# x's diagonals written by DMA, x's sums in h's rest banks, sums chained into h's rows, and four recurrence steps per turn of VectorE's loop

## The reference

```python
# 1. a recurrence over 128 time steps, batch 8, width 128, from h0 = cond_1024
xw = einsum('ntd,dh->nth', x, Wx) + b
h  = tanh(xw_t + h @ Wh)              # step by step
# 2. latent attention, 16 heads, causal, on h, added to x
# 3. a gated scan over time (adaptive layer) with softplus and tanh gates
# 4. six layers of local attention (16 heads of 64, window 32) and a gated feed-forward net
```

## Time and profile before

| | us |
|---|---|
| median of 3 runs | 3380.21 (3375.91 to 3382.81) |
| the profiled execution's own time | 3381.28 |
| its span | 3379.5 |
| PE busy | 2812.6 (83%) |
| VectorE busy | 2809.4 (83%) |
| ACT busy | 2171.9 (64%) |
| POOL busy | 2593.7 (77%) |

### The profile page before, as it was taken

One profiled execution on the slowest core, in us unless ns is written; L12 is line 12 of the kernel. 1 busy time (PEld: TensorE's weight loads), 2 busy tenths in 40 slices (PEclk: granted clock), 3 DMA queues, 4 the chain that ended last, 5 costly groups with the idle time before them and its releaser, 6 DMA issues.

```text
span 3379.5 us, 54177 instructions
## 1 busy us (share of the span) xinstructions
PE 2812.6 (83%) x12991; PEld 1717.5 (51%) x13101; DVE 2809.4 (83%) x8061; ACT 2171.9 (64%) x4492; POOL 2593.7 (77%) x2804
## 2 busy tenths in 40 slices
PE   5777778777787877878777788969999999999997
PEld 2333333333333333333333336746767777777676
DVE  5999999999999999999999994337777777777875
ACT  4666666666666666666666663336666666666665
POOL 8888888888888888888888881038778778778773
PEclk9999999999999999999999998879999999999999
DMA  1000000000000000000000002000010101000000
GB/s 33 0 0 0 0 0 0 0 0 0 0 0 0 0 0 0 0 0 0 0 0 0 0 0 73 1 1 1 0 36 0 36 0 36 0 32 4 0 0 7
DMA packets 21860, 21.97 MB, mean 7 GB/s; under 512 B 6334, under 2 KB 19396, under 8 KB 21060
## 3 DMA queue, kind: packets, MB, share of 16 engines
q1 hardware_dynamic: 21828, 21.55, 2.0%
HBM read 21.02 MB, written 0.52 MB: 6 GB/s over the span
## 4 chain that ended last, share of the span: by engine, by line
DVE 54%; PE 21%; issue 15%; ACT 4%; POOL 3%; DVEq 2%; SPq 0%; DMA 0%; POOLq 0%; ACTq 0%
DVE bank L1017 13%; PE bank L1322 5%; DVE bank L1012 3%; DVE bank L989 3%; DVE rot_s L1235 3%; DVE sq L989 3%; DVE rot_c L1235 3%; DVE ss L1238 3%; PE bank L1564 2%; DVE qT L998 2%; PE bank L1642 2%; DVE fix_trace L1083 2%; PE bank L1426 2%; PE bank L1616 2%; DVE sq L1075 2%
## 5 line engine op out<-in xcount | busy, mean ns | idle before, releaser
L1017 DVE TENSOR_REDUCE bank<-qkv_w 128x2 f32<-128x766 f32 (+1 forms) x768 | 912.7, 1219 | 120.6 <-issue 64.9
L739 ACT COPY qkv_w<-bank 128x512 f32<-128x512 f32 x258 | 218.2, 846 | 356.9 <-PE bank L1322 356.9
L667 POOL TENSOR_TENSOR qk<-rot_c,rot_s 128x512 f32<-128x512 f32 x192 | 256.8, 1337 | 207.8 <-DVE rot_s L1235 207.8
L1322 PE MATMUL bank<-diag_h,w_part 128*128 128x512 f32 x1024 | 307.2, 421 | 118.2 <-DVE bank L1012 106.9
L585 POOL TENSOR_TENSOR diag_h<-eye,part 128x512 fp32r<-128x512 f32 x384 | 393.9, 1040 | 0.0
L578 POOL TENSOR_TENSOR qkv_w<-b,offset 128x512 f32<-128x512 f32 x258 | 269.1, 1043 | 160.4 <-ACT b L721 150.0
L1327 PE MATMUL bank<-kT,wx 128*128 128x512 f32 x516 | 277.0, 618 | 136.3 <-ACT b L721 136.3
L1322 PE MATMUL bank<-diag_x,w_part 128*128 128x512 f32 x1032 | 385.6, 495 | 0.0
L1337 PE MATMUL bank<-qT,wh 128*128 128x256 f32 (+1 forms) x768 | 254.6, 467 | 95.6 <-DVE qT L998 95.6
L674 POOL TENSOR_TENSOR rs<-rs,halfs 128x8 f32<-128x8 f32 x192 | 320.1, 1667 | 16.0
L716 ACT ACTIVATE diag_x<-eye,X 128x128 fp32r<-128x128 f32 x1036 | 327.7, 389 | 1.4 <-DVE X L1110 1.4
(11 more groups left out here) (237 smaller groups left out, 6697.5 us busy)
## 6 DMA issues: line engine op xcount, KB each, us to landing
qkv_w<-in_L_ffn_Wqkv SPq DMA_DIRECT2D x6, 1536.0 KB
o_w<-in_L_ffn_Wo SPq DMA_DIRECT2D x6, 512.0 KB
w<-in_L_ffn_W SPq DMA_DIRECT2D x6, 341.0 KB
b<-in_L_ffn_b SPq DMA_DIRECT2D x6, 341.0 KB
w<-in_L_ffn_W SPq DMA_DIRECT2D x6, 128.0 KB
x_tok<-in_x SPq DMA_DIRECT2D x1, 512.0 KB
masks<-in_masks SPq DMA_DIRECT2D x1, 512.0 KB, 3.8
out<-o_fin SPq DMA_DIRECT2D x1, 512.0 KB, 3.2
```

The lines of the kernel that those rows point to most:

```text
L667: pool.tensor_tensor(o, c_, s_[:, :, ::-1, :], ALU.add).then_inc(rot_sum, 1)
L1017: return dve.tensor_reduce((sum_h, sum_x)[n][:, a:b], chain[n][:, a:b, 0:LINKS], AX_X, ALU.add)
L1322: return pe.matmul(dst, w_part[:, n, w], diag[n][:, d, a:b, :].rearrange("p n k -> p (n k)"), start=start, stop=stop or n == 0, skip_group ...
```

## The change

**x's diagonals by DMA.** ACT and POOL no longer make them. A ring of four slots in device memory holds, per slot, both parts' diagonal matrices for eight batch rows, 1 MB, cleared once with zeros from `o_fin`. In each step SyncE stores the 2 x 1024 elements of one later step of x onto the diagonals of a slot (a DMA with single elements of 4 bytes) and loads a half (512 KB, in 256 pieces of 2 KB) twice, each into its place in `diag_x` as soon as PE has done with it.

**Banks.** x's sums are made in banks 2 and 3, h's rest banks, when h's rests have been copied out of them. x's rests get a bank per half, 4 and 6. ACT reads a sum once into `guess_x` and once more, negated, into the rest bank, which takes the place of the product with `minus_eye`.

**Chained sums.** The bias is written once as the last link of x's rows; the result of x's fold is written as the last link of h's rows; folds read 384 in place of 383 links, and h's fold writes `pre` itself. The adds `xw` and `pre` go.

**Order and shares.** The triangle of h's batch rows 2, 3 moves from VectorE to ACT (`triangle_mid`). The lower diagonal of half 0 moves from ACT to POOL, that of half 1 from POOL to ACT. Both negated guesses of h are now POOL's (`minus_h`). PE makes all four products of half 0 before those of half 1.

**Loop.** VectorE's loop runs over 32 turns with four steps written out in each; the semaphore `rnn_op` is cleared once a turn.

```diff
+            def send_diagonals_x(step, slot):
+                for d in range(2):
+                    src = x_part[d][:, step, :] if isinstance(step, int) else x_part[d][:, bass.ds(step, 1), :].rearrange(
+                        "p a n -> p (a n)")
+                    dst = bass.AP(ring.tensor, (slot * P * 2 + d) * NB * D, [[2 * NB * D + 1, P], [D, NB], [1, 1]])
+                    sp.dma_start(dst, src.unsqueeze(2), allow_slow_non_contiguous=True).then_inc(diag_x_sent, 16)
+            def bring_diagonals_x(slot, half):
+                rows = slice(4 * half, 4 * half + 4)
+                sp.dma_start(diag[1][:, :, rows, :].bitcast(F32), ring[slot][:, :, rows, :]).then_inc(diag_x_ready[half], 16)
...
+            with sp.Fori(0, T // RING) as turn:
+                for u in range(RING):
+                    t = RING * turn + u
+                    sp.wait_ge(rest_ready[1], value(sp, 2 * t + 2))
+                    bring_diagonals_x((u + 1) % RING, 1)
+                    sp.wait_ge(rest_ready[1], value(sp, 2 * t + 3))
+                    bring_diagonals_x((u + 2) % RING, 0)
+                    sp.wait_ge(diag_x_sent, value(sp, 32 * t + 32 * RING))
+                    send_diagonals_x(value(sp, (t + RING) % T), u)
@@ POOL's loop @@
                 triangle(0, h_now[:], 1, tri_h_second)
                 pool.wait_ge(split_h, this)
-                for half in range(2):
-                    diagonal(0, 0, half, part[:, 0, 4 * half:4 * half + 4], diag_upper_h)
+                diagonal(0, 0, 0, part[:, 0, 0:4], diag_upper_h)
+                diagonal(0, 1, 0, part[:, 1, 0:4], diag_lower_h[0])
+                minus_h(0, counts[0])
+                diagonal(0, 0, 1, part[:, 0, 4:8], diag_upper_h)
                 pool.tensor_copy(hT[:, bass.ds(t, 1), :].rearrange("p a n -> p (a n)"), h_now[:]).then_inc(h_ready, 1)
-                diagonal(0, 1, 1, part[:, 1, 4:8], diag_lower_h[1])
-                pool.wait_ge(guess_placed, counts[1])
-                pool.tensor_tensor(adds[0][:, 4:8, :, 2], adds[0][:, 4:8, :, 1],
-                                   signs[:, 1:2].unsqueeze(2).to_broadcast([P, 4, D]), ALU.mult).then_inc(minus_placed[1], 1)
-                pool.wait_ge(rest_ready[1], counts[1])
-                diagonal(1, 1, 1, lower_x(around, 1), diag_x_ready[1])
+                minus_h(1, counts[1])
                 pool.wait_ge(x_scanned, this)
                 place_sums_x(0, counts[2])
                 place_sums_x(1, counts[3])
-                diagonal(1, 1, 0, lower_x(beyond, 0), diag_x_ready[1])
@@ ACT's loop @@
+            def triangle_mid():
+                for n in (2, 3):
+                    ins = act.activation(tri[0][:, n, :], upto[:], ACT.Copy, scale=h_now[:, n:n + 1])
+                ins.then_inc(tri_h_mid, 1)
             def take_sums_x(half, count):
+                act.activation(bank[:, REST_BANKS_X[half], :], sums_, ACT.Identity, bias=offset[:, 0:1],
+                               scale=-1.0).then_inc(less_guess, 1)
...
+                act.wait_ge(h_static, this)
+                triangle_mid()
                 place_guess_h(0, counts[0])
                 place_guess_h(1, counts[1])
                 act.wait_ge(split_h, this)
                 lower_h()
-                place_minus_h(counts[0])
                 place_rests_h(0, counts[0])
+                place_rests_h(1, counts[1])
                 act.wait_ge(sum_placed[1], counts[1])
+                act.wait_ge(rest_placed[1], counts[1])
                 take_sums_x(0, counts[2])
-                place_rests_h(1, counts[1])
                 take_sums_x(1, counts[3])
-                diagonals_x(around, 1)
                 act.wait_ge(x_scanned, this)
                 place_rests_x(0, counts[2])
-                diagonals_x(beyond, 0)
                 place_rests_x(1, counts[3])
@@ VectorE @@
-                return dve.tensor_reduce((sum_h, sum_x)[n][:, a:b], chain[n][:, a:b, 0:LINKS], AX_X, ALU.add)
+                return dve.tensor_reduce((pre, bias_at[0])[n][:, a:b], chain[n][:, a:b, :], AX_X, ALU.add)
...
-            with dve.Fori(0, T) as t:
+            with dve.Fori(0, T // UNROLL) as turn:
                 count[0] = 0
                 dve.sem_clear(rnn_op)
+                for u in range(UNROLL):
+                    t = UNROLL * turn + u
...
-                step(dve.tensor_scalar(xw[:], sum_x, rnn_b[:], None, ALU.add))
...
-                after(step(fold(0, 6, 8)))
-                after(tt(pre, xw[:], sum_h, ALU.add))
+                    after(n_h)
@@ PE's loop @@
-                sums_x(0, counts[2])
                 for half in range(2):
                     pe.wait_ge(diff_ready, counts[half])
+                    for d, made, count in ((0, diag_upper_h, counts[half]), (1, diag_lower_h[half], this)):
+                        pe.wait_ge(made, count)
+                        for w in range(2):
+                            ins = times(bank[:, REST_BANKS_H[half], :], 0, w, d, 4 * half, 4 * half + 4)
+                    ins.then_inc(rest_ready[0], 1)
+                for half in range(2):
+                    pe.wait_ge(rest_placed[0], quarters[half])
+                    sums_x(half, counts[2 + half])
                 offset_h()
+                for half in range(2):
+                    rests_x(half, counts[2 + half], landed)
```

More of the change, by code:

```diff
@@ L68 @@
 OFFSET = 12.0
-LINKS = 3 * D - 1
+UNROLL = 4
+RING = 4
 def constants():
@@ L237, in own @@
                                   **dict(zip(names[1:], shape[1:])))
-        sum_h, sum_x, pre = own(0, NB), own(0, NB), own(0, NB)
+        pre = own(0, NB)
         offset = sb("offset", [P, 2])
@@ L278, in program @@
         adds = [qkv_w[:, n, :].rearrange("p (n i c) -> p n i c", n=NB, c=3) for n in range(2)]
+        bias_at = [tile[:, :, D - 1, 2] for tile in adds]
         chain = [qkv_w[:, n, :].rearrange("p (n i) -> p n i", n=NB) for n in range(2)]
+        ring = nc.dram_tensor('diag_ring', (RING, P, 2, NB, D), F32, kind='Internal').ap()
         in_x = sem("in_x")
@@ L304, in program @@
         guess_placed = sem("guess_placed_h")
-        minus_placed = [sem("minus_placed_h%d" % half) for half in range(2)]
+        minus_placed = sem("minus_placed_h")
         diag_upper_h = sem("diag_upper_h")
         diag_lower_h = [sem("diag_lower_h%d" % half) for half in range(2)]
-        diag_x_ready = [sem("diag_upper_x"), sem("diag_lower_x")]
+        diag_x_ready = [sem("diag_x%d" % half) for half in range(2)]
+        zeros_ready = sem("zeros_ready")
+        diag_x_sent = sem("diag_x_sent")
+        ring_clear = sem("ring_clear")
         tri_h_first = sem("tri_h_first")
@@ new lines, in _, with placed_h @@
+                dve.sem_clear(rnn_op)
+                for u in range(UNROLL):
+                    t = UNROLL * turn + u
+                    this, two = value(dve, t + 1), value(dve, 2 * t)
+                    counts = [value(dve, two + n) for n in (1, 2, 3, 4)]
+                    quarters = [value(dve, 4 * t + n) for n in (1, 2, 3, 4)]
+                    def placed_h(m):
+                        dve.wait_ge(rest_placed[0], quarters[m])
+                        if m % 2 == 0:
+                            dve.wait_ge(minus_placed, counts[m // 2])
+                    placed_x(counts[0])
+                    n_x = step(fold(1, 0, 4))
+                    for half in range(2):
+                        difference_h(half, counts[half])
+                    placed_x(counts[1])
+                    fold(1, 4, 8).then_inc(x_scanned, 1)
+                    after(n_x)
+                    for m in range(4):
+                        placed_h(m)
+                        if m == 2:
+                            dve.wait_ge(x_scanned, this)
+                        n_h = step(fold(0, 2 * m, 2 * m + 2))
+                    after(n_h)
+                    tanh()
+                    open_step(value(dve, t + 2))
@@ L1339, in sums_h, with rests_x @@
                                  skip_group_check=True)
[L1341 removed]
+            def rests_x(half, count, landed):
                 a, b = 4 * half, 4 * half + 4
[L1343 removed]
+                at = bank[:, REST_BANKS_X[half], :]
                 rows = at.rearrange("p (n k) -> p n k", k=D)
                 pe.wait_ge(guessed, count)
[L1346 to L1347 removed]
+                pe.wait_ge(less_guess, count)
+                pe.matmul(rows, eye[:], guess_x[:, a:b, 0:D], start=False, stop=True, skip_group_check=True)
+                pe.wait_ge(diag_x_ready[half], landed)
                 for d in range(2):
[L1349 to L1351 removed]
+                    for w in range(2):
+                        ins = times(at, 1, w, d, a, b)
                 ins.then_inc(rest_ready[1], 1)
```

155 lines of the change are left out of this document (60 added, 95 removed).

## The result

The changed kernel takes **3302.0 us** (median of 4 runs, 3298.6 to 3307.7), beside 3381.5 for the kernel before on the same chip: ratio 0.976 [0.975, 0.978]. That is 79.5 us off, where 142 were forecast (143 less 1 for the start), and 2 us above the range. The sign was right; 62 us are missing.

The account below looks back on a forecast made before the run. VectorE, busy 94% of the loop, was taken to bound the kernel: 128 steps each 1.12 us shorter (143) off 3381.3, plus 1 for start and end, gave 3239, or 3238 us against the median; 8-in-10 range 3212 to 3300.

Parts of the forecast that it names:

- Off VectorE's path go the products by -eye: TensorE's products by -eye, 1.0 us a half, and diagonals leave other engines; worth nothing by itself, pays for x's longer line.
- x's side, 0.3 us to spare: x's longer line through ScalarE, GpSimd and TensorE: GpSimd's and ScalarE's work each ends 0.3 us before it is needed.
- The rival (3295): x's side or ScalarE takes over through negated copies and ten handovers 0.03 us worse: steps of 15.0, 3295 us; chance 0.20.
- VectorE's sum: VectorE's list in one step: adds, triangle, stall and turn save 1.33 us; 14.55 on average once its wait is counted.
- The wait for the guess: Before h's first difference, VectorE waits 0.26 us for ScalarE's guess in three steps of four.
- The turn: VectorE's loop turn comes once in four steps: gain 0.43 us in three of four, 0.32 on average.
- The negated copy: ScalarE's negated copy of x's guess, PSUM to PSUM: bounds 0.69 and 0.96 us, 0.69 taken.
- The DMA: Loads of 1 MB (3.1 us) and 2048 single-element stores (2) a step: 5 of 14.5 us, hidden, so 0.
- The start: Before the loop, clears and chained stores end near 45 us: 0 to 5 us once; +1 for start and end.
- The loop body: Rival: each of VectorE's 32 loop turns waits 0 to 2.3 us for an instruction block: 3275 us; chance 0.07.

Follow-up runs that it names:

- e1: The changed kernel with 4 matmuls added behind h's sums and 5 behind x's rests in each step: 3254.2 us, ratio 0.962.
- e11: The changed kernel with 2 matmuls added behind h's sums and 2 behind x's rests in each step: 3249.0 us, ratio 0.961.
- e8: The changed kernel with -guess again from TensorE's product with the negative identity, not from ScalarE's second copy: 3307.2 us, ratio 0.978.
- e9: e1 with the triangle of h's elements 2 and 3 back on VectorE: 3261.3 us, ratio 0.965.
- e7: e1 with one step in each turn of VectorE's loop instead of four: 3266.9 us, ratio 0.966.
- e3: The changed kernel without the loop's stores of 4-byte elements, fetches kept: 3303.4 us, ratio 0.977.
- e13: e6 without the loop's stores and fetches of x's diagonals, TensorE waiting for the first landing alone: 3232.9 us, ratio 0.956.
- e4: The changed kernel with the zeros of all four ring slots written before the loads of the attention's weights: 3294.9 us, ratio 0.975.
- e6: e1 and e4 together, against the changed kernel: 3241.8 us, ratio 0.959.

## Why the prediction was wrong, point by point

- **The clock: the step that failed.** Every duration in the sum was a row at full clock, and the earlier trace rows showed 1.00. The prediction wrote "Off VectorE's path go the products by -eye" and put the exchange at nothing. It was worth the clock: TensorE idled 32.0 us in the ten steps of the earlier trace rows, 3.2 of 15.67, in four pieces of at most 1.06; in the step shown above it is 1.72 + 1.13 + 0.72 = 3.6 of 14.53, although its last products ran at half rate. The price was 54 us, which e1 and e11 took back, and with the product back there was no stretch (e8). That matmuls with short idle times between groups can make the clock swing is in the Trainium skill ("TensorE: Matmul & The Clock Gate", A second HAM failure mode: psum-queue depth-cycling); the trace agrees, with idle times of 0.7 to 1.7 us between groups. It was the rule to weigh here, but it would not have settled the forecast: the kernel before idles between its groups too, 0.46 to 1.06, and its clock never fell in the loop.
- **x's side, 0.3 us to spare.** Right for neither engine: in a step of e1 ScalarE is done 0.55 us before it is wanted and GpSimd 0.1 (its triangles of x end at 1022.60, h's begins at 1022.70). That GpSimd has so little is the reason why the clock cost anything. The rival (3295) named the place that gave way, but held ten late handovers responsible. At full clock there were none (e1: VectorE's folds of x do not wait for ScalarE's copies); with the product back, its mechanism is real (e8, 14.93 beside its 15.0).
- **VectorE's sum.** Forecast 14.52 in three steps of four and 14.66 with the turn; e1 has 14.46 and 14.67, 14.516 on average against 14.55. The two adds and the stall ahead of h's folds are gone.
- **The wait for the guess.** 0.26 forecast. From x's fold to L1046 it is 1.93 us (1021.66 to 1023.59), against 1.67 for such a fold with nothing behind it: 0.26. e9 shows the other side: of the triangle's 0.33 this wait takes back all but 0.03 (0.07 by the prediction's terms), except in the turn's step.
- **The turn.** Gain 0.43 for VectorE alone, 0.14 of the step net of the wait; e7 measured 0.19.
- **The negated copy.** 0.69 taken, 0.65 measured, the value below both bounds.
- **The DMA.** 5 us of the queues' time a step forecast, 5.2 measured; hidden (e3, e13). The times to landing were too low: 6.1 us for a half and 5.4 for a store are the medians of the page after, where 3.8 and 3.3 were taken. The three of them in a row would be 17.6 us, over the 12 that were allowed; yet in the loop TensorE never waits for a fetch.
- **The start.** +1 us taken for start and end, 0 to 5 allowed, 8 measured. The mis-sized term is the end of the other slots' clears and chained stores: put near 45 us, the clears issued at 28.32 hold the stores until 42.22, these end at 51.9, and the fetch behind them is issued at 52.02. e4 took back 7, a part of it by the clock (see e6).
- **The loop body.** The count was right at four steps; its cost past the edge, bounded at 2.3 us a turn, is 3.9.

## What to carry to other kernels

Before work is taken off TensorE in a loop of short dependent steps, look at its idle times and at the granted clock: work that costs nothing on the path may be what keeps the clock up. A row at full clock is no promise for the kernel after the change. Where the clock falls for short stretches, look where in the step they begin and put a few cheap matmuls into every gap that precedes one; filling one gap of two gained 0 and 14 us here, filling both thinly gained 53. And unroll only as far as the loop body stays loaded: from four steps to eight the turn went from 0.2 us to 4.

## What the runs showed of the hardware that was not expected

- Stretches at 1.2 GHz came though TensorE was busy for 76% of the loop (1294.81 of 1700) and its longest idle time since the same place of the step before was 1.7 to 2.0 us in 46 of 48 cases (2.3 and 2.8 in the other two); most lasted 3.4 us and cost the kernel 1.1 us each.
- Where the work stands counts, not only how much: 4 added matmuls in one gap left 42 stretches, 5 in the other 28, 2 and 2 in the two gaps one.
- A loop body of eight steps brought 0.76 MB more of instructions over its 16 turns, and VectorE waited some 4 us at each of them (61.1 us in all).
